# One pass of ScalarE and a rounding copy on VectorE in place of two passes of ScalarE, in a mixture-of-experts kernel

## The chip, the cores and the metric

The kernel runs as one program on one core of a Trainium2 chip. The metric is the device time of the whole program in microseconds (us); lower is better. Beside it stands the span, which is the time from the first to the last instruction in the profiled execution. Five engines work side by side, each through its own list in order: TensorE (PE; its weight loads are shown apart as PEld), VectorE (DVE), ScalarE (ACT), GpSimd (POOL) and SyncE (SP). They wait for each other through semaphores.

## The reference

A modulated linear layer is followed by a mixture of experts with residual. There are T = 8192 tokens with D = 256 features, E = 8 experts with F = 1024 hidden units, the two best experts of each token are taken, and each expert takes at most 2560 tokens.

```python
ys = y * scale
d = jax.lax.rsqrt(jnp.einsum('bi,io->bo', ys * ys, weight * weight) + EPS)
out = jnp.einsum('bsi,io->bso', Efou * ys[:, None, :], weight) * d[:, None, :]
...
logits = x @ wr.T
vals, idx = jax.lax.top_k(logits, TOP_K)
...
xg = x_pad[dispatch]
h = _gelu(jnp.einsum('ecd,edf->ecf', xg, w1) + b1[:, None, :])
y = jnp.einsum('ecf,efd->ecd', h, w2) + b2[:, None, :]
g = g_pad[dispatch, jnp.arange(E)[:, None]]
wy = y * g[..., None]
```

## The kernel before, in words

The first 100 us or so compute the modulated layer and the routing for 16 groups of 512 tokens. Then come 52 blocks, each for one expert. A long block has 3 x 128 gathered tokens (384 columns), a short one 2 x 128 (256 columns). The first blocks, of expert 0, are all long; each later expert has some long blocks and then some short ones. The whole document calls the change from the last long block of an expert to its first short block a seam. There are seven seams, one for each of experts 1 to 7, and their first short blocks start at about 252, 353, 471, 560, 648, 767 and 873 us.

All products run on TensorE in the type fp32r. To keep accuracy a matrix is split in two parts, hi (the value rounded to fp32r) and lo (the value less hi). The hidden layer of a block is made in 8 chunks of 128 hidden units, f = 0 to 7. For each chunk:

- PE makes the first product into one of two PSUM banks, `h_bank` (lines 611 to 613, 6 matmuls), and signals `h_open`.
- ACT (`gelu`, line 853) turns the bank into `h_raw` in full fp32, and once more into `h_hi`, rounded to fp32r. After both it signals `gelu_done`. This lets PE write the bank again (`bank_read`) and lets DVE go on.
- DVE (`split_chunk`, line 1262) computes `h_lo` as `h_raw` less `h_hi`, and signals `h_ready`.
- PE makes the second product with `h_hi` and `h_lo` as stationary operands (lines 625 and 627, in blocks 0 and 1 lines 642 to 645) once `chunk_split` has seen `h_ready`. `h_raw`, `h_hi` and `h_lo` are rings of four.

PE runs ahead: it makes the first product of chunk f before the second product of chunk f - 3, and it opens chunks 0 and 1 of the next block before it ends this one. The order of each engine is written out by hand. On DVE the work between two blocks is: chunk 7 of this block, chunk 0 of the next, then for each 128 tokens an addition of PSUM and bias and a second addition (lines 1290 and 1293, which wait for PE's `y_done` and free PE's output banks through `y_read`), then chunk 1 of the next block, then one multiplication by the gate for each 128 tokens (line 1299, `y_ready`), then chunks 2 to 7. After chunk 6 DVE makes the lo part of the next block's input (line 1247) and copies the gates (line 1256). Chunks 0 and 1 of a block are always split over 384 columns there, also when the block is short. In the first two long blocks of an expert DVE also splits the next expert's weights (line 982) between chunks 2 to 5.

GpSimd gathers the tokens of a later block (line 417), and adds the weighted results to the output in DRAM with indirect DMAs (line 438) after `y_ready`. The landing of those DMAs (`added`) is awaited by the next block's first line 1290.

In block 0 DVE still has routing work between the chunks. It makes the last choice of experts (to line 1025), then chunk 0, the gates (lines 1030 to 1034), chunk 1, the slots (lines 1046 to 1151, which wait for a product of PE), chunk 2, a one-hot list (lines 1076 to 1097), chunks 3 and 4, and so on.

Of the kernel before, what the change touches and what calls it, by code (L numbers as in the profile page):

```python
# [13 lines left out]
ACT = mybir.ActivationFunctionType  # L14
AX_X = mybir.AxisListType.X

P = 128
# [5 lines left out]
FC = F // P  # L23
# [48 lines left out]
RING = 4  # L72
H_BANKS = 2
# [13 lines left out]
def build(nc, x, x_t, cond_t, w, wr_t, w1, b1_t, w2, b2, ident, tri, expert_low, slot_base, middle_ids, lanes, columns,  # L87
# [9 lines left out]
    with ExitStack() as ctx:  # L97
        def sb(name, shape, dt=F32):
            return ctx.enter_context(nc.sbuf_tensor("sb_" + name, shape, dt))

        def sem(name):
            return ctx.enter_context(nc.semaphore(name))
# [19 lines left out]
        b1_now = [sb(f"b1_now{u}", [P, FC]) for u in range(2)]  # L122
# [68 lines left out]
        h_raw = [h_raw_sb[:, i * SLOTS:(i + 1) * SLOTS] for i in range(RING)]  # L191
        h_hi = [sb(f"h_hi{i}", [P, SLOTS], F32R) for i in range(RING)]
# [101 lines left out]
        gelu_done = sem("gelu_done")  # L294
        h_ready = sem("h_ready")
        y_done = sem("y_done")
        y_half = sem("y_half")
        y_read = sem("y_read")
        y_ready = sem("y_ready")
        added = sem("added")  # L300
# [21 lines left out]
        h_bank = [bank[4], bank[5]]  # L322
# [443 lines left out]
        def _(act):  # L766
# [82 lines left out]
            def gelu(u, b, f, subs=SUBS):  # L849

                act.wait_ge(h_open, b * FC + (f + 1))
                for h in (h_raw[f % RING], h_hi[f % RING]):
                    ins = act.activation(h[:, 0:subs * P], h_bank[f % H_BANKS][:, 0:subs * P], ACT.Gelu_apprx_tanh,  # L853
                                         bias=b1_now[u][:, f:f + 1])
                ins.then_inc(gelu_done, 1)

            def one_block(u, e, b, piece0, last=False, subs=SUBS):
                for f in range(FC):
                    gelu(u, b, f, subs)
                    if isinstance(b, int) and b == 0 and f == 1:  # L860
                        odds(SETS - 1)
                    if f == 6 and not last:
                        act.wait_ge(h_open, b * FC + FC)
                        split_rows(b + 1)
                    if piece0 is not None and f in SPLIT_AT:
                        split_piece(1 - u, piece0 + SPLIT_AT.index(f), 32 * (e + 2))
# [34 lines left out]
        def _(dve):  # L901
# [356 lines left out]
            def split_chunk(b, f, subs=SUBS):  # L1258

                cols = slice(0, subs * P)  # L1260
                dve.wait_ge(gelu_done, b * FC + (f + 1))
                dve.tensor_tensor(h_lo[f % RING][:, cols], h_raw[f % RING][:, cols],  # L1262
                                  h_hi[f % RING][:, cols].bitcast(F32), ALU.subtract).then_inc(h_ready, 1)

# [3 lines left out]
            take_gates(0, first=True)  # L1268
            choose(SETS - 1)
            split_chunk(0, 0)  # L1270
            set_gates(SETS - 1)
            split_chunk(0, 1)
            find_slots(SETS - 1)
            list_third_block()
# [40 lines left out]
            def one_block(u, e, b, piece0, last=False, subs=SUBS):  # L1315

                for f in range(2, FC):
                    split_chunk(b, f, subs)
                    if isinstance(b, int) and b < 2 and f in (2, 4):
                        list_group(LAST_SET + 2 * b + f // 2 - 1)  # L1320
                    if isinstance(b, int) and b == 1 and f == 5:
                        base_of_slots()
                    if f == 6 and not last:
                        split_rows(b + 1)
                        take_gates(b + 1, first=isinstance(b, int) and b == 0)
                    if piece0 is not None and f in SPLIT_AT:
                        i = piece0 + SPLIT_AT.index(f)
                        split_piece(1 - u, i, PIECES * (e + 1) + (i + 1))
                if isinstance(b, int) and b == 1:
                    plan_blocks()  # L1330
                if not last:
                    split_chunk(b + 1, 0)
                if isinstance(b, int) and b == 0:
                    dve.wait_ge(b2_in, 16)
                for s in range(subs):
                    if last:
                        last_sum(e, b, s, subs)
                    else:
                        add_bias(e, b, s, subs)
                if not last:  # L1340
                    split_chunk(b + 1, 1)
                    for s in range(subs):
                        weigh(e, b, s, subs)
# [80 lines left out]
```

## Time and profile before

| what | value |
|---|---|
| time, median of 3 runs | 905.96 us (905.81 to 906.36) |
| time of the profiled execution | 906.11 us |
| its span | 904.0 us |
| around the span | 2.1 us |
| granted TensorE clock over the span | 0.997 |
| busy share PE / PEld / DVE / ACT / POOL | 99 / 89 / 59 / 60 / 49 % |
| start of the first block's second products | 113.9 us (chunk 2), 116.6 us (chunk 3) |

The profiled execution's own time is the span and the 2.1 us around it. Busy time of an engine is the union of its instructions, so two that overlap in the pipeline count once. A share of 99% on PE says that PE almost always has a matmul in flight.

### The profile page before, as it was taken

Reading aid. Unit: us, or ns where it says so; the run is one execution under the profiler, and the core shown is the slowest. Engines: PE = TensorE matmul, PEld = TensorE weight load, DVE = VectorE, ACT = ScalarE, POOL = GpSimd, SP = SyncE. Lnnn points to the kernel's source line nnn. Section 1 sums busy time; section 2 is a strip of 40 time slices with the busy share of each in tenths; the row PEclk is TensorE's granted clock in tenths of the full one; section 3 lists DMA queues with packets and bytes.
Section 4 is the critical chain, followed back from the end, with each engine's and each line's share of the span. In section 5 each row is a group of like instructions: output and inputs, shape, how many; then the busy total and the mean of one; then the engine's idle time right before and its main releaser. Section 6 shows DMA issues by size and latency. Waiting matters only on the chain.

```text
span 904.0 us, 18417 instructions
## 1 busy us (share of the span) xinstructions
PE 892.1 (99%) x5605; PEld 807.3 (89%) x5605; DVE 532.2 (59%) x1286; ACT 541.2 (60%) x1290; POOL 445.2 (49%) x472
## 2 busy tenths in 40 slices
PE   9999999999999999999999999999999999999995
PEld 6666899999999999999999999999999999999995
DVE  5789876556455565565455555556456645544543
ACT  4888645656556665666556655666566645655552
POOL 0000324645466545665446654655566544664453
PEclk9999999999999999999999999999999999999998
DMA  9775582522533353333423352335233322342232
GB/s 334 260 255 186 181 298 44 133 62 43 133 54 57 52 139 44 57 64 57 122 42 59 60 133 42 62 54 140 39 57 66 46 44 42 52 67 36 47 42 30
DMA packets 55848, 84.37 MB, mean 93 GB/s; under 512 B 6848, under 2 KB 44880, under 8 KB 55408
## 3 DMA queue, kind: packets, MB, share of 16 engines
q0 software_dynamic: 28592, 38.20, 26.6%
q1 hardware_dynamic: 25632, 44.87, 14.7%
q10 hardware_dynamic: 1568, 0.58, 0.2%
q8 instruction: 32, 0.52, 0.2%
q14 instruction: 24, 0.20, 0.1%
HBM read 53.71 MB, written 38.31 MB: 102 GB/s over the span
## 4 chain that ended last, share of the span: by engine, by line
PE 97%; ACT 1%; DMA 1%; DVE 0%; POOLq 0%; issue 0%; POOL 0%; SPq 0%; ACTq 0%
PE bank L625 26%; PE bank L611 14%; PE bank L612 14%; PE bank L613 14%; PE bank L627 13%; PE bank L514 6%; PE bank L599 3%; PE bank L527 2%; PE bank L529 2%; PE bank L562 1%; PE bank L642 1%; PE bank L644 1%; PE bank L645 1%; DMA sb_x<-in_x_t 1%; POOLq L97 0%
## 5 line engine op out<-in xcount | busy, mean ns | idle before, releaser
L625 PE MATMUL bank<-sb_w_both,sb_h_hi 128*128 128x512 f32 x1000 | 373.8, 402 | 0.0
L853 ACT ACTIVATE sb_h_raw<-bank,sb_b_now 128x384 f32<-128x384 f32 (+1 forms) x416 | 223.6, 538 | 249.4 <-PE bank L613 248.7
L1262 DVE TENSOR_TENSOR sb_h_lo<-sb_h_raw,sb_h_hi 128x384 fp32r<-128x384 f32 (+1 forms) x416 | 209.6, 511 | 226.1 <-ACT sb_h_hi L853 224.3
L438 POOL DMA_INDIRECT out_rows<-sb_y,sb_add_ids x154 | 271.3, 1762 | 125.8 <-DVE sb_y L1299 85.2
L627 PE MATMUL bank<-sb_w_both,sb_h_lo 128*128 128x256 f32 x1000 | 282.1, 282 | 0.0
L611 PE MATMUL bank<-sb_xt_hi,sb_w_both 128*128 128x384 f32 (+1 forms) x832 | 264.6, 318 | 0.2 <-ACT sb_h_hi L853 0.2
L612 PE MATMUL bank<-sb_xt_lo,sb_w_both 128*128 128x384 f32 (+1 forms) x832 | 260.1, 313 | 0.0
L613 PE MATMUL bank<-sb_xt_hi,sb_w_both 128*128 128x384 f32 (+1 forms) x832 | 259.8, 312 | 0.0
L853 ACT ACTIVATE sb_h_hi<-bank,sb_b_now 128x384 fp32r<-128x384 f32 (+1 forms) x416 | 221.0, 531 | 0.0
L625 PEld LDWEIGHTS bank<-sb_w_both,sb_h_hi 128*128 128x128 f32 x1000 | 188.0, 188 | 30.2 <-DVE sb_y L1293 0.2
L627 PEld LDWEIGHTS bank<-sb_w_both,sb_h_lo 128*128 128x128 f32 x1000 | 188.5, 189 | 0.0
L611 PEld LDWEIGHTS bank<-sb_xt_hi,sb_w_both 128*128 128x128 f32 x832 | 156.7, 188 | 20.3 <-DVE sb_xt_lo L1247 0.8
L417 POOL DMA_INDIRECT sb_xg<-hidden,sb_gather_ids x133 | 136.7, 1028 | 70.9 <-POOL sb_ids_ring L413 43.5
L612 PEld LDWEIGHTS bank<-sb_xt_lo,sb_w_both 128*128 128x128 f32 x832 | 156.8, 189 | 0.0
L613 PEld LDWEIGHTS bank<-sb_xt_hi,sb_w_both 128*128 128x128 f32 x832 | 156.4, 188 | 0.0
L410 POOL COPY sb_gather_ids<-sb_ids 128x3 int32 (+2 forms) x52 | 9.9, 190 | 247.5 <-DVE sb_gates L1256 127.7
L1247 DVE TENSOR_TENSOR sb_xt_lo<-bank,sb_xt_hi 128x384 fp32r<-128x384 f32 x104 | 53.1, 552 | 73.4 <-ACT sb_xt_hi L828 73.4
L828 ACT CAST sb_xt_hi<-bank 128x384 fp32r<-128x384 f32 x104 | 44.8, 483 | 78.1 <-PE bank L613 76.4
L1290 DVE TENSOR_TENSOR sb_y<-bank,sb_b 128x256 f32<-128x256 f32 x125 | 52.4, 420 | 31.8 <-PE bank L627 26.8
L514 PE MATMUL bank<-sb_x,sb_w 128*128 128x512 f32 x128 | 57.7, 595 | 0.4 <-DVE sb_x L931 0.4
L1293 DVE TENSOR_TENSOR sb_y<-sb_y,bank 128x256 f32<-128x256 f32 x125 | 52.6, 421 | 5.8
L982 DVE TENSOR_TENSOR sb_w_both<-sb_w_raw,sb_w_both 128x512 fp32r<-128x512 f32 x64 | 44.0, 688 | 3.5 <-ACT sb_w_both L796 3.4
(148 smaller groups left out, 620.7 us busy)
## 6 DMA issues: line engine op xcount, KB each, us to landing
sb_w_raw<-in_w SPq DMA_DIRECT2D x16, 1024.0 KB, 9.6
hidden<-sb_rows SPq DMA_DIRECT2D x4, 2112.0 KB, 10.3
sb_x<-in_x_t SPq DMA_DIRECT2D x16, 512.0 KB, 5.7
out_rows<-in_x SPq DMA_DIRECT2D x16, 512.0 KB, 7.5
out_rows<-sb_y,sb_add_ids POOLq DMA_INDIRECT x155, 3.9
sb_xg<-hidden,sb_gather_ids POOLq DMA_INDIRECT x133, 2.8
sb_b<-in_b SPq DMA_DIRECT2D x1, 1024.0 KB, 9.7
hidden<-sb_empty SPq DMA_DIRECT2D x4, 132.0 KB, 8.0
```

The costliest lines, as they stand in the source:

```text
L417: pool.indirect_dma_start(xg[:, s, :], None, hidden[0:PAD + sets * TS * P, :], bass.IndirectOffsetOnAxis(gather_ids[:, s:s + 1], axis=0),) ...
L438: pool.indirect_dma_start(out, bass.IndirectOffsetOnAxis(add_ids[:, s:s + 1], axis=0), y[s][:, :], None, compute_op=ALU.add,).then_inc(add ...
L514: mm = pe.matmul(m_bank[c % M_RING][:, :], w_sb[:, k, o * P:(o + 1) * P], x_in[g % X_RING][:, k, :], start=(k == 0), stop=(k == KC - 1))
L611: pe.matmul(h, w_hi[u][:, cols], xt_hi[:, rows], start=(k == 0), stop=False)
L612: pe.matmul(h, w_hi[u][:, cols], xt_lo[:, rows], start=False, stop=False)
L613: mm = pe.matmul(h, w_lo[u][:, cols], xt_hi[:, rows], start=False, stop=(k == KC - 1))
L625: pe.matmul(wide_bank[s][:, :].rearrange("p (v d) -> p v d", v=2), hi, w_both[u][:, :, cols], start=(f == 0), stop=False, skip_group_check ...
L627: mm = pe.matmul(wide_bank[s][:, 0:D], lo, w_hi[u][:, cols], start=False, stop=(f == FC - 1), skip_group_check=True)
L853: ins = act.activation(h[:, 0:subs * P], h_bank[f % H_BANKS][:, 0:subs * P], ACT.Gelu_apprx_tanh, bias=b1_now[u][:, f:f + 1])
L1247: dve.tensor_tensor(xt_lo[:, rows_k], x_bank[k][:, 0:SLOTS], xt_hi[:, rows_k].bitcast(F32), ALU.subtract).then_inc(xt_ready, 1)
L1262: dve.tensor_tensor(h_lo[f % RING][:, cols], h_raw[f % RING][:, cols], h_hi[f % RING][:, cols].bitcast(F32), ALU.subtract).then_inc(h_read ...
L1293: dve.tensor_tensor(y[s][:, :], y[s][:, :], wide_bank[s][:, D:2 * D], ALU.add).then_inc(y_read, signals(s, subs))
```

## The change

In `gelu` ScalarE makes one pass in place of two. It writes `h_raw` alone and signals `gelu_done` after it. In `split_chunk` VectorE first copies `h_raw` into `h_hi`, which rounds it to fp32r, and signals a new semaphore `hi_made`. It waits for this semaphore itself and then takes the difference as before. Nothing else is changed; the lines behind the new ones move by one.

```diff
         y_half = sem("y_half")
+        hi_made = sem("hi_made")
         y_read = sem("y_read")
...
                 act.wait_ge(h_open, b * FC + (f + 1))
-                for h in (h_raw[f % RING], h_hi[f % RING]):
-                    ins = act.activation(h[:, 0:subs * P], h_bank[f % H_BANKS][:, 0:subs * P], ACT.Gelu_apprx_tanh,
-                                         bias=b1_now[u][:, f:f + 1])
-                ins.then_inc(gelu_done, 1)
+                act.activation(h_raw[f % RING][:, 0:subs * P], h_bank[f % H_BANKS][:, 0:subs * P], ACT.Gelu_apprx_tanh,
+                               bias=b1_now[u][:, f:f + 1]).then_inc(gelu_done, 1)
...
                 dve.wait_ge(gelu_done, b * FC + (f + 1))
+                dve.tensor_copy(h_hi[f % RING][:, cols], h_raw[f % RING][:, cols]).then_inc(hi_made, 1)
+                dve.wait_ge(hi_made, b * FC + (f + 1))
                 dve.tensor_tensor(h_lo[f % RING][:, cols], h_raw[f % RING][:, cols],
                                   h_hi[f % RING][:, cols].bitcast(F32), ALU.subtract).then_inc(h_ready, 1)
```

On DVE, between two blocks, the program has these rows before: the last pair of additions, chunk 1 of the next block, and the multiplications by the gates.

```order
L1290 TENSOR_TENSOR sb_y<-bank,sb_b 128x256 [waits y_done]
L1293 TENSOR_TENSOR sb_y<-sb_y,bank 128x256 [waits y_half]
L1261 REGISTER_ALU
L1262 TENSOR_TENSOR sb_h_lo<-sb_h_raw,sb_h_hi 128x384 [waits gelu_done]
L1298 REGISTER_ALU
L1299 ISA [waits y_read]
L1299 TENSOR_SCALAR sb_y<-sb_y,sb_gates 128x256
```

After the change the same place of the same engine reads so; the copy is listed as CAST.

```order
L1291 TENSOR_TENSOR sb_y<-bank,sb_b 128x256 [waits y_done]
L1294 TENSOR_TENSOR sb_y<-sb_y,bank 128x256 [waits y_half]
L1260 REGISTER_ALU
L1261 CAST sb_h_hi<-sb_h_raw 128x384 [waits gelu_done]
L1263 TENSOR_TENSOR sb_h_lo<-sb_h_raw,sb_h_hi 128x384 [waits hi_made]
L1299 REGISTER_ALU
L1300 ISA [waits y_read]
L1300 TENSOR_SCALAR sb_y<-sb_y,sb_gates 128x256
```

One instruction is put in ahead of each difference, with no further register instruction, and what follows on DVE stands behind both.

## Rows read from the trace of the kernel before

**Rows 1.** The page: busy time by engine, and the chain that ended last.
```profile
PE 892.1 (99%) x5605; PEld 807.3 (89%) x5605; DVE 532.2 (59%) x1286; ACT 541.2 (60%) x1290; POOL 445.2 (49%) x472
...
PE 97%; ACT 1%; DMA 1%; DVE 0%; POOLq 0%; issue 0%; POOL 0%; SPq 0%; ACTq 0%
```

**Rows 2.** The page's groups, ScalarE's two passes: busy us, mean ns, idle before.
```profile
L853 ACT ACTIVATE sb_h_raw<-bank,sb_b_now 128x384 f32<-128x384 f32 (+1 forms) x416 | 223.6, 538 | 249.4 <-PE bank L613 248.7
...
L853 ACT ACTIVATE sb_h_hi<-bank,sb_b_now 128x384 fp32r<-128x384 f32 (+1 forms) x416 | 221.0, 531 | 0.0
```

**Rows 3.** Groups of VectorE by shape, over the whole span.
```profile
L1262 DVE TENSOR_TENSOR sb_h_lo<-sb_h_raw,sb_h_hi 128x384 fp32r<-128x384 f32 x278 | 153.2, 556 | 168.4 <-ACT sb_h_hi L853 167.3 <-issue 0.2 <-DVE sb_rows L1034 0.2
L1262 DVE TENSOR_TENSOR sb_h_lo<-sb_h_raw,sb_h_hi 128x256 fp32r<-128x256 f32 x138 | 56.4, 423 | 57.7 <-ACT sb_h_hi L853 57.1
...
L1299 DVE TENSOR_SCALAR sb_y<-sb_y,sb_gates 128x256 f32<-128x256 f32 x131 | 40.1, 356 | 0.0
...
L914 DVE TENSOR_SCALAR sb_ys_t<-sb_ys_t 128x256 f32<-128x256 f32 x1 | 0.3, 294 | 3.0 <-DMA sb_ys_t<-in_cond_t 3.0
...
L976 DVE CAST sb_tri<-sb_tri_f 128x128 bf16<-128x128 f32 x1 | 0.2, 219 | 0.0
```

**Rows 4.** Timeline of VectorE in block 0: start us, us, what.
```profile
108.49 0.56 DVE L1262 TENSOR_TENSOR sb_h_lo<-sb_h_raw,sb_h_hi 128x384 fp32r<-128x384 f32 x1 [0.15 <-DVE sb_rows L1034]
109.58 0.29 DVE L1046 TENSOR_SCALAR sb_over<-bank 128x128 f32<-128x128 f32 x1 [0.53 <-PE bank L548]
...
113.26 0.55 DVE L1262 TENSOR_TENSOR sb_h_lo<-sb_h_raw,sb_h_hi 128x384 fp32r<-128x384 f32 x1
...
115.69 1.02 DVE L1262 TENSOR_TENSOR sb_h_lo<-sb_h_raw,sb_h_hi 128x384 fp32r<-128x384 f32 x2
```

**Rows 5.** Timeline, block 0, first weight load of chunks 2 and 3.
```profile
113.86 0.19 PEld L642 LDWEIGHTS bank<-sb_w_both,sb_h_hi 128*128 128x128 f32 x1 [0.33 <-DVE sb_h_lo L1262]
...
116.64 0.19 PEld L642 LDWEIGHTS bank<-sb_w_both,sb_h_hi 128*128 128x128 f32 x1
```

**Rows 6.** Timeline of VectorE at the second seam.
```profile
352.54 0.42 DVE L1290 TENSOR_TENSOR sb_y<-bank,sb_b 128x256 f32<-128x256 f32 x1
352.99 0.42 DVE L1293 TENSOR_TENSOR sb_y<-sb_y,bank 128x256 f32<-128x256 f32 x1
353.33 0.55 DVE L1262 TENSOR_TENSOR sb_h_lo<-sb_h_raw,sb_h_hi 128x384 fp32r<-128x384 f32 x1
353.80 0.87 DVE L1299 TENSOR_SCALAR sb_y<-sb_y,sb_gates 128x256 f32<-128x256 f32 x3
354.58 0.42 DVE L1262 TENSOR_TENSOR sb_h_lo<-sb_h_raw,sb_h_hi 128x256 fp32r<-128x256 f32 x1
```

**Rows 7.** Timeline, second seam, first weight load of chunks 1 and 2.
```profile
354.20 0.19 PEld L625 LDWEIGHTS bank<-sb_w_both,sb_h_hi 128*128 128x128 f32 x1
...
355.61 0.19 PEld L625 LDWEIGHTS bank<-sb_w_both,sb_h_hi 128*128 128x128 f32 x1
```

**Rows 8.** Timeline at the first seam, chunk 1: VectorE, then its weight load.
```profile
252.85 0.55 DVE L1262 TENSOR_TENSOR sb_h_lo<-sb_h_raw,sb_h_hi 128x384 fp32r<-128x384 f32 x1
...
253.57 0.19 PEld L625 LDWEIGHTS bank<-sb_w_both,sb_h_hi 128*128 128x128 f32 x1
```

**Rows 9.** Timeline, short block behind a short block, chunk 1 likewise.
```profile
364.92 0.55 DVE L1262 TENSOR_TENSOR sb_h_lo<-sb_h_raw,sb_h_hi 128x384 fp32r<-128x384 f32 x1
...
366.13 0.19 PEld L625 LDWEIGHTS bank<-sb_w_both,sb_h_hi 128*128 128x128 f32 x1
```

**Rows 10.** Timeline, last add behind the second seam; the line 1290 that awaits it.
```profile
359.04 1.57 POOL L438 DMA_INDIRECT out_rows<-sb_y,sb_add_ids  x1 [0.30 <-issue]
...
363.27 0.42 DVE L1290 TENSOR_TENSOR sb_y<-bank,sb_b 128x256 f32<-128x256 f32 x1 [0.33 <-PE bank L627]
```

**Rows 11.** The page's DMA issues: count, median us from issue to landing.
```profile
out_rows<-sb_y,sb_add_ids POOLq DMA_INDIRECT x155, 3.9
```

**Rows 12.** Timeline, a gather's issue under two of line 1299.
```profile
791.24 0.65 DVE L1299 TENSOR_SCALAR sb_y<-sb_y,sb_gates 128x256 f32<-128x256 f32 x2
...
791.29 0.95 POOL L417 DMA_INDIRECT sb_xg<-hidden,sb_gather_ids  x1 [0.30 <-issue]
```

## The prediction

> **What bounds the kernel now.** I first read the busy shares and the chain of waits. PE has a matmul in flight for 99% of the span and holds 97% of the chain; ACT and DVE hold 1% or less of it, though each is busy for 60% [rows 1]. So what ACT saves is worth nothing by itself. PE never waits for `gelu_done` except once near 106 us, for about 0.3 us, before other waits end. The change can only matter where it makes PE wait. So the second thing I read, block by block, is how long before the first weight load of each second product its `h_lo` is ready. I call this the slack of the chunk. The weight load is the place to look, since it loads `h_hi`, the part that `chunk_split` guards.
>
> Most slacks are large: 0.9 to 5 us. Three kinds of place are tight, all where DVE has other work in a row, so that chunks stand in its queue with their activation long done:
>
> - Block 0. Chunk 2 is ready at 113.26 + 0.55 = 113.81, and PE loads at 113.86 after an idle 0.33 us that DVE ended: PE already waits there. It starts 0.04 us after the release, which I use as the time to wake up. The pair of chunks 3 and 4 begins at 115.69, so chunk 3 is ready at about 116.25, against a load at 116.64: slack 0.39 [rows 4, 5].
> - The seams. Chunk 1 stands behind six additions. At the second seam it is ready at 353.33 + 0.55 = 353.88 against 354.20: slack 0.32. Chunk 2 is ready at 355.00 against 355.61: slack 0.61 [rows 6, 7]. At the first seam chunk 1 has 253.57 - 253.40 = 0.17 [rows 8]. The other five are like the second to within 0.05 us.
> - A short block behind a short one: chunk 1 has 366.13 - 365.47 = 0.66 [rows 9], the same in all of them, and chunk 2 some 1.2.
>
> **The change part by part.** ACT loses 416 passes, 221.0 us [rows 2]. That is off PE's path. Where DVE waits for ACT, the chunk's latency hardly moves: the second pass goes (0.53 us of record, some 0.1 less in the pipeline) and a copy of nearly that length comes. These are the 226 us in which DVE now idles for `h_hi` [rows 3], so there the copy is hidden in the time that ACT gives back. Where the activation is long done and DVE is behind, as in the three places above, the whole copy is added.
>
> The price of the copy. No row has an fp32 copy of 384 columns. One bound is two elements a cycle: a scaling in SBUF takes 294 ns for 256 columns, and a cast 219 for 128 [rows 3]. That is 75 ns for 128 columns more, so 384 columns are some 0.36 us. The other bound is the rate of the two-operand difference, 556 ns for 384 and 423 for 256 [rows 3]. I take 0.36 and 0.29, because the copy is like the cast and the scaling: one source, both sides in SBUF. The difference then waits for the copy's own semaphore. The pair of lines 1290 and 1293 shows such a wait: 352.54 + 0.42 = 352.96, and the next starts at 352.99 [rows 6], so 0.03 to 0.05. The sum is **0.40 us for a chunk of 384 columns, 0.33 for 256** (by the other bound 0.60 and 0.46). DVE gets 278 x 0.40 + 138 x 0.33 = 157 us more work and stays below 80% busy.
>
> The Trainium skill has the same on the rate ("VectorE: DVE Perf Modes", the perf-mode tier table): a copy from SBUF to SBUF in fp32 runs at two elements a cycle, a tensor_tensor at one. It says nothing of fp32r as the output type.
>
> Term 1, block 0. Chunks 0 and 1 get a copy each, 0.80. The difference of chunk 1 ends at 109.05, and DVE then idles 0.53 us for PE before line 1046 (0.61 from where it could start, as operations behind each other overlap by 0.08) [rows 4]. So the slots start 0.80 - 0.61 = 0.2 later. The copy of chunk 2 adds 0.40, so PE waits 0.6 longer for chunk 2. Chunk 3 becomes ready 0.2 + 0.4 + 0.4 = 1.0 later, and with its slack of 0.39 and the waking this moves PE to 1.0 - 0.39 + 0.04 = 0.65 in all. Chunks 4 to 7 have over 2 us and absorb the rest. **+0.65 us.**
>
> Term 2, the seams. At the second one chunk 1 is ready 0.40 later: 0.40 - 0.32 + 0.04 = 0.12 of waiting. The three multiplications behind it move by 0.40 too, and chunk 2 has a copy of 256: 0.73 later, 0.73 - 0.61 + 0.04 = 0.16 in all. Chunk 3 has about 2 us. So 0.16 for six seams, and 0.40 - 0.17 + 0.04 = 0.27 for the first (with its chunk 2: 0.33). 6 x 0.16 + 0.33 = **+1.3 us.**
>
> Costed at nothing: the short blocks (0.40 against 0.66; if the copy cost 0.60 its cover would be just gone), the additions of lines 1290 and 1293, which wait for PE after an idle of 0.33 [rows 10] while chunk 0's chain stays as long as it was, and the copy in the last block, where it takes the place of a pass. `y_ready` comes 0.40 later because the multiplications stand behind chunk 1. GpSimd's adds wait for it, and the next line 1290 for their landing. This is closest behind a seam: the last add is issued at 359.04 and lands 3.9 later (median), at 362.94, against 363.27 [rows 10, 11]. That is 0.33, and PE has itself moved by 0.16, so 0.40 just fits. I add **0.1** for this and for the first gather behind the block plan, which PE meets with about 0.1 to spare.
>
> Sum: 0.65 + 1.3 + 0.1 = 2.05 us. The profiled execution took 906.11 (span 904.0), 0.15 above the median of 905.96, so the sum gives 908.16 from the one and 908.0 from the other; I forecast **908.1 us**. About 0.2% (1.8 us) is what a measurement of this kernel can tell from no change, so the forecast stands close to that line, on its slower side.
>
> **The rivals.**
>
> A, not slower: the copy is covered nearly whole. Three of line 1299 take 0.87 [rows 6], so such operations start 0.26 apart. If the difference could start 0.26 behind the copy and not 0.40, block 0 would cost 0.26 (two copies, 0.52, stay below the 0.61), the seams nothing (0.26 against 0.32 and 0.46 against 0.61), and the first seam 0.13. Sum 0.4: 906.5 us. It decides at about 0.30 for the copy and its wait. Against it: the dependent pair 1290 and 1293 starts only after the end.
>
> B, the copy runs at one element a cycle, because its output is fp32r: 0.60 and 0.46. Block 0: 1.2 - 0.61 + 0.6 = 1.2 at chunk 2, and 1.8 - 0.39 + 0.04 = 1.45 at chunk 3. A seam: 1.06 - 0.61 + 0.04 = 0.5, the first 0.65, in all 3.65. With 0.3 for the plan's gather the sum is 5.4: 911.5 us. Against it are the cast and the scaling of [rows 3]; for it only that none of them writes fp32r.
>
> C, the copies hold up GpSimd. If its DMAs could not be issued while a copy runs, the three adds behind a seam (about 5.5 us, some four copies of 0.29) would end 1.2 us later, plus the 0.40 of `y_ready`. Less the 0.33 the next line 1290 is 1.2 us late, and PE stands still for nearly all of that, since its output banks come free late. Seven seams: 8 us more, 916 us. The row nearest to it speaks against it: a gather's issue under 0.65 us of two scalings took 0.95 [rows 12], which is as short as such an issue gets.
>
> The Trainium skill ("SBUF — State Buffer", SBUF: two separate sides) states the rule behind C: an operation of DVE in a two-port mode, as an fp32 copy in SBUF is, locks GpSimd out of the shared port, and it can then write no descriptors. By that rule line 1299 should lengthen the issue, and here it doesn't.
>
> **How the numbers follow.** The forecast has 0.60, A 0.12, B 0.14, C 0.10; 0.04 is left for something that makes it faster by over 0.2%, for which I see no mechanism, as PE is at work throughout. The forecast's own range is 907.1 to 909.2, by 0.3 or 0.45 for the copy and its wait. It crosses the line of 907.8, and I put 0.2 of its 0.60 below. Same: 0.20 + 0.12 + 0.02 = 0.34. Slower: 0.40 + 0.14 + 0.08 = 0.62. The range that holds 8 in 10 reaches from A to B, 906.5 to 911.7, and leaves out C and the faster rest.
>
> **What would show it.** The copy's group should have 278 of some 0.36 us and 138 of 0.29, ACT's busy time should fall by 220 us and DVE's rise by about 150. The list of waits should have PE's weight loads waiting for `h_lo` at 114 and 117 us and at the seams, in all 1 to 2 us more, and nowhere else. A copy of 0.55 would say B; issues of line 438 longer than now, or line 1290 waiting for landings at seven places, would say C. I am wrong altogether if PE's matmuls change their pace, or if waits turn up in the short blocks.

## The result, and the profile after

The changed kernel takes 910.53 us (median of 4 runs, 910.52 to 911.22) against 905.91 us for the kernel before (4 runs, 905.81 to 906.36): a ratio of 1.005, with a 95% interval of 1.0039 to 1.0062. It is 4.6 us slower. The profiled execution has a span of 908.4 us against 904.0, 4.4 us more, at a granted clock of 0.996.

The page, with the busy time by engine and the chain that ended last, answers to [rows 1]:

```profile
PE 895.3 (99%) x5605; PEld 809.2 (89%) x5605; DVE 670.7 (74%) x1702; ACT 367.4 (40%) x874; POOL 437.4 (48%) x472
...
PE 92%; DVE 3%; issue 2%; DMA 1%; ACT 1%; POOLq 0%; POOL 0%; DVEq 0%; ACTq 0%
...
L853 ACT ACTIVATE sb_h_raw<-bank,sb_b_now 128x384 f32<-128x384 f32 (+1 forms) x416 | 223.0, 536 | 403.7 <-PE bank L614 403.7
```

ACT lost 173.8 us of busy time and not 221: passes that ran into each other were counted once where they overlapped. DVE gained 138.5 us. PE's share of the chain fell from 97% to 92%. The groups of VectorE by shape answer to [rows 3]:

```profile
L1263 DVE TENSOR_TENSOR sb_h_lo<-sb_h_raw,sb_h_hi 128x384 fp32r<-128x384 f32 x278 | 156.4, 563 | 9.6
L1261 DVE CAST sb_h_hi<-sb_h_raw 128x384 fp32r<-128x384 f32 x278 | 104.9, 377 | 74.0 <-ACT sb_h_raw L853 68.9 <-issue 4.7 <-DVE sb_rows L1033 0.2
...
L1261 DVE CAST sb_h_hi<-sb_h_raw 128x256 fp32r<-128x256 f32 x138 | 43.4, 315 | 10.8 <-ACT sb_h_raw L853 8.2 <-issue 1.2
```

The copy is a CAST in the trace. It takes 377 and 315 ns in the mean, 0.35 and 0.29 us where nothing disturbs it. The two-operand difference takes 0.56 and 0.43, so the copy runs at the faster of the two rates that the prediction weighed, as forecast. "issue" is idle time that no wait explains; the difference had 0.2 us of it before, the copy has 5.9.

To find where 4.4 us went I took, for each block, the first weight load of chunk 0's second product, and compared it with the same load before:

| stretch | change, us | forecast |
|---|---|---|
| start of the span to block 0 | -0.56 | 0 |
| block 0 | +1.09 | +0.65 |
| blocks 1 and 2 (the gather behind the plan) | +0.16 | 0.1 with `y_ready` |
| seven seams: 0.31, 0.30, 0.47, 0.31, 0.30, 0.59, 0.40 | +2.68 | +1.3 |
| short blocks 9 to 11 | +0.36 | 0 |
| blocks 44, 45 | +0.21 | 0 |
| all other blocks (none over 0.03) | 0.0 | 0 |
| last block to the end | +0.46 | 0 |

The second seam on VectorE, against [rows 6]:

```profile
354.32 0.42 DVE L1294 TENSOR_TENSOR sb_y<-sb_y,bank 128x256 f32<-128x256 f32 x1
354.66 0.35 DVE L1261 CAST sb_h_hi<-sb_h_raw 128x384 fp32r<-128x384 f32 x1
355.05 0.56 DVE L1263 TENSOR_TENSOR sb_h_lo<-sb_h_raw,sb_h_hi 128x384 fp32r<-128x384 f32 x1
355.52 0.87 DVE L1300 TENSOR_SCALAR sb_y<-sb_y,sb_gates 128x256 f32<-128x256 f32 x3
356.44 0.29 DVE L1261 CAST sb_h_hi<-sb_h_raw 128x256 fp32r<-128x256 f32 x1
356.77 0.43 DVE L1263 TENSOR_TENSOR sb_h_lo<-sb_h_raw,sb_h_hi 128x256 fp32r<-128x256 f32 x1
```

Chunk 1 is as forecast: its difference starts 355.05 - 354.66 = 0.39 later than it would. Then look at what starts behind the multiplications. They end at 355.52 + 0.87 = 356.39, and the copy starts at 356.44, 0.05 after. In [rows 6] the next operation starts at 354.58, 0.09 *before* the end at 354.67. Of a seam's 0.31, chunk 1 has 0.13 and chunk 2 has 0.18, where the forecast had 0.12 and 0.04. So about 0.14 a seam is time that no instruction of the sum accounts for.

PE's weight loads by what they waited for (total us, times, longest; waits under 0.15 are not listed, so most of the seams don't show):

```profile
PEld bank L643 <- DVE sb_h_lo L1263: 1.8, 2, 1.3
...
PEld bank L612 <- DVE sb_xt_lo L1246: 1.6, 8, 0.4
...
PEld bank L626 <- DVE sb_h_lo L1263: 0.7, 3, 0.3
```

The first line is block 0: two waits of 1.8 together, where the kernel before had two of 0.9. The second is for the lo part of the next block's input; its longest, 0.4, stands in block 43 and comes up again below.

### The profile page after: what moved, and what is told of

Its sections match the earlier page's. It is cut to its first block, busy times and chain, and to the rows that moved or that the text cites. A ratio compares the mean times of both kernels' runs of the same rounds, so it can differ in the third digit from the quotient of the medians.

```text
span 908.4 us, 18417 instructions
## 1 busy us (share of the span) xinstructions
PE 895.3 (99%) x5605; PEld 809.2 (89%) x5605; DVE 670.7 (74%) x1702; ACT 367.4 (40%) x874; POOL 437.4 (48%) x472
## 4 chain that ended last, share of the span: by engine, by line
PE 92%; DVE 3%; issue 2%; DMA 1%; ACT 1%; POOLq 0%; POOL 0%; DVEq 0%; ACTq 0%
PE bank L626 26%; PE bank L612 13%; PE bank L628 13%; PE bank L613 13%; PE bank L614 13%; PE bank L515 6%; PE bank L600 3%; PE bank L528 2%; PE bank L530 2%; PE bank L563 1%; PE bank L495 1%; DVE sb_h_lo L1263 0%; DMA out_rows<-sb_y,sb_add_ids 0%; DMA sb_xg<-hidden,sb_gather_ids 0%; POOLq L97 0%
## 5 line engine op out<-in xcount | busy, mean ns | idle before, releaser
L439 POOL DMA_INDIRECT out_rows<-sb_y,sb_add_ids x154 | 257.6, 1672 | 133.6 <-DVE sb_y L1300 93.0
L1263 DVE TENSOR_TENSOR sb_h_lo<-sb_h_raw,sb_h_hi 128x384 fp32r<-128x384 f32 (+1 forms) x416 | 215.5, 518 | 14.3
L1261 DVE CAST sb_h_hi<-sb_h_raw 128x384 fp32r<-128x384 f32 (+1 forms) x416 | 148.3, 357 | 84.8 <-ACT sb_h_raw L853 77.0
L418 POOL DMA_INDIRECT sb_xg<-hidden,sb_gather_ids x133 | 139.4, 1048 | 70.9 <-POOL sb_ids_ring L414 43.5
```

Of the source, the lines that this page charges most:

```text
L418: pool.indirect_dma_start(xg[:, s, :], None, hidden[0:PAD + sets * TS * P, :], bass.IndirectOffsetOnAxis(gather_ids[:, s:s + 1], axis=0),) ...
L439: pool.indirect_dma_start(out, bass.IndirectOffsetOnAxis(add_ids[:, s:s + 1], axis=0), y[s][:, :], None, compute_op=ALU.add,).then_inc(add ...
L1261: dve.tensor_copy(h_hi[f % RING][:, cols], h_raw[f % RING][:, cols]).then_inc(hi_made, 1)
```

## The experiments

My theory after the result: (1) the copy costs only where VectorE is already late, and not by how many copies there are; (2) at a seam it costs 0.4 us of work, less the slack, and 0.14 more, because the difference waits for an instruction of VectorE itself: that holds its sequencer, which then can't do the loop's bookkeeping for chunk 2 ahead of time; (3) the tail's 0.46 comes from `y_ready`. All runs are compared with the kernel before on the same chip; its medians there were 906.49, 906.23 and 906.41.

**e1, chunk 1 back on ScalarE.**

```diff
+                for h in (h_raw[f % RING], h_hi[f % RING]) if f == 1 else (h_raw[f % RING],):
...
+                if not (f == 1):
+                    dve.tensor_copy(h_hi[f % RING][:, cols], h_raw[f % RING][:, cols]).then_inc(hi_made, 1)
+                    dve.wait_ge(hi_made, b * (FC - 1) + max(f, 1))
```

> The changed kernel, but ScalarE again makes both passes for chunk 1 of every block (no copy and no wait on hi_made there); the other seven chunks keep the copy. Theory: of the 4.4 us that the change cost, 2.7 came at the seven seams and 0.5 at the tail, and both come from the copy of chunk 1 that stands behind the additions (it makes chunk 1 and y_ready 0.40 late and takes VectorE's head start before chunk 2). Then the seams cost at most 0.5 together, the last landing is waited for no longer than before (0.16 us), and the time is about 907.2 (906.6 to 907.8). Rival: the copies cost by how many there are (work on VectorE, use of SBUF), wherever they stand; with 52 of 416 gone only an eighth of 4.4 us comes back, about 910.0.

Measured 907.07 us (10 runs), ratio 1.0009 (0.9999 to 1.0018), span 904.9. All seven seams cost 0.00, blocks 9 to 11, 44 and 45 nothing either, and the last block -0.04. Block 0 and the stretch ahead of it come to +0.18. What is left is block 2, which grew by 0.69, and block 3 by 0.15: PE's transposes waited for the gather behind the plan. So one copy in eight made most of the loss, 3.4 of the 4.4 us by the profiles, and the count theory (910.0) is out. The multiplications behind chunk 1 and the first copy of chunk 2:

```profile
354.79 0.87 DVE L1303 TENSOR_SCALAR sb_y<-sb_y,sb_gates 128x256 f32<-128x256 f32 x3
355.58 0.29 DVE L1264 CAST sb_h_hi<-sb_h_raw 128x256 fp32r<-128x256 f32 x1
```

355.58 is 0.08 before their end at 355.66. With neither the copy nor the self-wait ahead of it, the overlap is back; e1 alone can't tell which of the two took it.

**e2, block 0 back on ScalarE.** The condition is `isinstance(b, int) and b == 0` in place of `f == 1`; in block 0 ScalarE's first pass counts `hi_made` up in the copy's place.

> The changed kernel, but ScalarE makes both passes in block 0 only. Theory: block 0 lost 1.09 us against its own start, through the copies of chunks 0 to 3 in front of and between the slot plan's operations; without them that comes back and everything behind it moves 0.6 to 1.1 us earlier: 909.4 to 909.9 us, with the seams as in the changed kernel. Rival: PE's wait in block 0 has another end behind it (the gathers of the plan), and the gain is given back by block 3: 910.3 to 910.6.

Measured 909.56 us, ratio 1.0038 (1.0024 to 1.0052), span 907.4: inside the theory's interval. Block 0 grew by 0.01, but block 2, with PE's wait for its gather, grew by 0.34 where the changed kernel had 0.21. The seams cost 0.31 to 0.34 but for block 23's 0.67, and the last block 0.55.

**e3, the kernel before with a wait of VectorE on itself.**

```diff
                 dve.wait_ge(gelu_done, b * FC + (f + 1))
+                dve.memset(tiny_sb[:, :], 0.0).then_inc(tiny_made, 1)
+                dve.wait_ge(tiny_made, b * FC + (f + 1))
```

> The kernel before, but VectorE writes one column (a memset of 128x1 that nothing reads) ahead of each difference, and the difference waits for that memset's own semaphore. It adds the wait on VectorE itself with hardly any of the copy's work. Theory: a wait on an instruction of VectorE itself holds its sequencer, so that the loop's bookkeeping before chunk 2 starts only when chunk 1's difference has been sent; then chunk 2's first instruction starts up to 0.1 us after the end of the multiplications and no longer 0.08 before it, and the seams cost 0.05 to 0.15 us each; time 906.2 to 907.5. Rival: the extra at chunk 2 comes from the copy's length; then chunk 2's first instruction still starts 0.08 before the end and each seam is as before to within 0.03 beyond what the memset itself lasts, time 905.9 to 906.4.

Measured 907.07 us (10 runs), ratio 1.0006 (0.9996 to 1.0015), span 904.5. The time can't be told from that of the kernel before; what follows rests on the trace. The second seam:

```profile
353.37 0.06 DVE L1264 MEMSET sb_tiny<- 128x1 f32 x1
353.48 0.56 DVE L1266 TENSOR_TENSOR sb_h_lo<-sb_h_raw,sb_h_hi 128x384 fp32r<-128x384 f32 x1
353.95 0.87 DVE L1303 TENSOR_SCALAR sb_y<-sb_y,sb_gates 128x256 f32<-128x256 f32 x3
354.91 0.06 DVE L1264 MEMSET sb_tiny<- 128x1 f32 x1
```

The multiplications end at 354.82, and the next operation starts at 354.91, 0.09 after the end, where it was 0.09 before the end. Work of 0.06 us did that, so it isn't the copy's length. That it isn't the additional instruction either is for e7 to show. The gap is 0.07 to 0.09 at five seams and 0.18 to 0.20 at two, those of blocks 23 and 50. In the changed kernel it is 0.04 to 0.06 at five and 0.17 and 0.15 at the same two, which is why these cost 0.47 and 0.40 there. In the kernel before it was -0.08, and -0.05 once. Counted over the seven seams the changed kernel lost 1.1 us of head start. Here the seams themselves cost 0.01 to 0.07 each, less than I expected: chunk 2's difference ends 355.43 - 353.00 = 2.43 behind the start of the last addition, where it was 355.00 - 352.99 = 2.01, and the slack of 0.61 covers these 0.42. The rest of the 0.5 us by which this profile is longer stands in block 0 (0.18), blocks 18 and 19 (0.18) and the last block (0.12).

**e7, the copy of chunk 1 ahead of the last pair of additions.** `round_chunk` is the copy with its wait for `gelu_done`; the wait on `hi_made` stays ahead of the difference.

```diff
                 for s in range(subs):
+                    if not last and s == subs - 1:
+                        round_chunk(b + 1, 1, slice(0, SUBS * P))
...
-                    split_chunk(b + 1, 1)
+                    split_chunk(b + 1, 1, rounded=True)
```

> The changed kernel, but chunk 1's copy is issued before the last pair of additions instead of behind it; the work on VectorE is the same and the copy still stands in the same row, only its semaphore is long up when chunk 1's difference comes. Theory of the sequencer: chunk 1 is as late as in the changed kernel, but VectorE's head start is back, chunk 2's copy starts 0.08 before the end of the multiplications, and each seam costs about 0.15 less: 909.4 us (909.0 to 909.8). Rival: the loss at the seams is the copy's length alone and no matter of order: 910.3 to 910.7.

Measured 912.95 us, ratio 1.0073 (1.0056 to 1.009), span 910.8: slower than the changed kernel, which neither side expected. Yet the seams did what the theory says, and more: 0.03 to 0.09 at five of them in place of about 0.31, and 0.34 and 0.33 at blocks 43 and 50.

```profile
355.91 0.42 DVE L1299 TENSOR_TENSOR sb_y<-sb_y,bank 128x256 f32<-128x256 f32 x1
356.25 0.55 DVE L1268 TENSOR_TENSOR sb_h_lo<-sb_h_raw,sb_h_hi 128x384 fp32r<-128x384 f32 x1
356.72 0.87 DVE L1305 TENSOR_SCALAR sb_y<-sb_y,sb_gates 128x256 f32<-128x256 f32 x3
357.51 0.29 DVE L1260 CAST sb_h_hi<-sb_h_raw 128x256 fp32r<-128x256 f32 x1
```

The copy starts 0.08 before the end of the multiplications at 357.59: the head start is back, with the same instructions in the row and no wait that is still open in front of the difference. The loss is elsewhere. Block 2 grew by 1.07, since the three issues of its gather took 1.42, 1.30 and 1.29 (more on this under e5). Fifteen short blocks grew by 0.2 to 0.5 each, and PE's weight loads there waited for the last addition:

```profile
PEld bank L626 <- DVE sb_y L1299: 4.7, 15, 0.4
```

I had counted the slack of `h_lo` and not that of the additions. In short blocks it is smaller than the copy is long.

The sequencer's own records at the second seam, first the kernel before, then the changed one, e3 and e7 (counts, min/median/max ns, first and last start):

```profile
L1299 DVEq FUSED_REGOPS  x3: 65/71/140, 353.2 to 353.7; - x3
```
```profile
L1300 DVEq FUSED_REGOPS  x3: 65/71/140, 355.1 to 355.7; - x3
```
```profile
L1303 DVEq FUSED_REGOPS  x3: 65/71/140, 353.6 to 354.1; - x3
```
```profile
L1305 DVEq FUSED_REGOPS  x3: 65/71/140, 356.0 to 356.6; - x3
```

The first register operation comes 0.6 us ahead of the first multiplication before (353.2 against 353.80), 0.4 in the changed kernel (355.1, 355.52), 0.35 in e3 (353.6, 353.95) and 0.7 in e7 (356.0, 356.72). This lead is what the self-wait takes and the early copy gives back. Behind the multiplications come the registers and the branch of the loop. In the changed kernel the last of them is the second of these two, which starts at 356.34 and lasts 0.06; the copy of chunk 2 starts at 356.44, 0.05 after its end:

```profile
L1352 DVEq FUSED_REGOPS  x2: 63/120/177, 356.1 to 356.3; - x2
```

The record at which the lead begins shows the same. In the kernel before, the sequencer's record for the first multiplication starts 0.21 us ahead of the difference (353.12 against 353.33). In the changed kernel the sequencer's first record behind the difference starts 0.01 us after the difference itself has started (355.06 against 355.05), so it stood still while the difference waited for the copy.

**e4, the copy at the rate of the difference.**

```diff
-                dve.tensor_copy(h_hi[f % RING][:, cols], h_raw[f % RING][:, cols]).then_inc(hi_made, 1)
+                dve.tensor_tensor(h_hi[f % RING][:, cols], h_raw[f % RING][:, cols], h_raw[f % RING][:, cols],
+                                  ALU.max).then_inc(hi_made, 1)
```

> The changed kernel with the copy replaced by a tensor_tensor of the same result (the larger of h_raw and h_raw), which takes one element per cycle: 0.56 us for 384 columns and 0.43 for 256 instead of 0.36 and 0.29. Theory (what counts is how late VectorE is where it is late already): at each seam 0.20 + 0.14 more, so 0.6 to 0.7 per seam instead of 0.35, block 0 0.4 to 0.6 more, some short blocks begin to wait: 913.5 to 916 us. And if the copies in the changed kernel are lengthened by a port that VectorE shares with GpSimd, this operation, which needs both sources and never leaves GpSimd out, is lengthened differently: its records beside GpSimd's instructions are within 0.03 us of those without. Rival: PE has cover for another 0.2 us, 910.5 to 911.5.

Measured 916.57 us, ratio 1.0113 (1.0097 to 1.0128), span 915.0. The groups by shape:

```profile
L1261 DVE TENSOR_TENSOR sb_h_hi<-sb_h_raw 128x384 fp32r<-128x384 f32 x278 | 154.1, 554 | 53.5 <-ACT sb_h_raw L853 48.9 <-issue 4.2 <-DVE sb_rows L1033 0.2
...
L1261 DVE TENSOR_TENSOR sb_h_hi<-sb_h_raw 128x256 fp32r<-128x256 f32 x138 | 57.8, 419 | 3.5 <-ACT sb_h_raw L853 1.3 <-issue 0.8
```

Six seams cost 0.62 to 0.76 and block 43's has 0.96, blocks 0 to 2 together 3.26. So 0.20 us more on each copy of 384 columns and 0.13 on one of 256 made 6 us more, slightly over what I expected. The mean of 554 ns is that of the undisturbed difference, 556 [rows 3]. The 83 of these operations that lay wholly within an issue of GpSimd took 0.55 to 0.59, those beside none 0.55 to 0.56, so this form is hardly lengthened. The additional 0.03 at most is just what the expectation allowed.

**e5, e1 and e2 together.** The condition is `f == 1 or (isinstance(b, int) and b == 0)`; 357 copies are left (not 317, as I wrote below before the run).

> The two undone parts together: ScalarE makes both passes in block 0 and for chunk 1 of every block, the copy does the rest (317 of 416 chunks). Theory: the copies that are left stand where VectorE waits for ScalarE, so they cost nothing: as the kernel before, 905.9 to 906.6 us, with no wait of PE for h_lo beyond the kernel before's. Rival: the parts overlap and block 3 (the first gather behind the block plan) gives 0.3 to 0.8 back: 906.6 to 907.2.

Measured 906.98 us (11 runs), ratio 1.0009 (1.0 to 1.0018): the rival's number, not the theory's. Block 0 grew by 0.07 and the seams by nothing, but block 2 grew by 0.73. (Two later blocks, 16 and 39, have a jump of 0.33 each, of the kind described under b2.) The three issues of the gather behind the plan, and VectorE's copies at the same time:

```profile
148.64 1.42 POOL L418 DMA_INDIRECT sb_xg<-hidden,sb_gather_ids  x1 [0.84 <-POOL sb_ids_ring L414]
150.36 1.30 POOL L418 DMA_INDIRECT sb_xg<-hidden,sb_gather_ids  x1 [0.30 <-issue]
151.97 1.29 POOL L418 DMA_INDIRECT sb_xg<-hidden,sb_gather_ids  x1 [0.30 <-issue]
...
149.66 0.55 DVE L1266 CAST sb_h_hi<-sb_h_raw 128x384 fp32r<-128x384 f32 x1
...
151.33 0.51 DVE L1266 CAST sb_h_hi<-sb_h_raw 128x384 fp32r<-128x384 f32 x1
```

Both sides are lengthened: the copies by 0.16 to 0.20, and the issues, which took 1.19, 1.10 and 0.95 in the kernel before, in sum by 0.77.

**e8, the early copy only in long blocks.** The condition of e7 becomes `early and s == subs - 1`, with `early = subs == SUBS and not isinstance(b, int)`.

> The changed kernel, but chunk 1's copy stands before the last pair of additions only where the loop over long blocks issues it (so at the seams too), and behind them in short blocks and in blocks 0 and 1. The version with the early copy everywhere had the seams at 0.07 us each but every short block 0.2 to 0.3 later, because PE waited there for the last additions. Theory: seams 0.07 and short blocks as in the changed kernel, in sum 1.7 us less than the changed kernel: about 908.8 us (908.4 to 909.2). Rival: the delay of the additions shows behind the long blocks too, or the next block gives the seam's gain back: 910 us or more.

Measured 908.79 us, ratio 1.0026 (1.0016 to 1.0037), as the theory gave. Four seams cost 0.03 to 0.05 and two 0.09; block 43 has 0.32, block 9 keeps its 0.29 and the last block has 0.66. This is 1.7 us faster than the changed kernel with the same work on every engine.

**e10, the change in the first chunk alone.** The kernel before, with one pass and a copy for chunk 0 of block 0.

> The kernel before with the change in one chunk alone, chunk 0 of block 0, where PE waits for ScalarE's second pass (0.5 us by the list of waits) and VectorE has 0.6 us idle behind it. Theory: the start of block 0's second products moves 0.2 to 0.4 us earlier and block 0 keeps it, 905.5 to 905.8 us, which only the trace can tell from the kernel before. Rival: the slot plan behind it is 0.4 later and PE gives it all back in block 0: 905.9 to 906.1.

Measured 906.39 us against 906.23, ratio 1.0002 (0.9993 to 1.0011). Block 1 started 0.16 us earlier, which is about what two profiles of one kernel differ by (0.09, below). It beats nothing that can be measured.

**e11, no copy beside that gather.** e5, with `b < 3` in place of `b == 0`.

> The version with both parts undone, and ScalarE also makes both passes in blocks 1 and 2, so that no copy stands beside the first gather behind the block plan (block 3's, issued during block 2). Theory: a copy beside a gather's issue lengthens both; the three issues of that gather take 3.2 us again as in the kernel before, not 4.0, PE waits for it less than 0.2 us, and block 3 starts as in the kernel before: 906.1 to 906.4 us, 0.6 to 0.8 less than with copies in blocks 1 and 2. Rival: the gather starts late for another reason (the index copy of GpSimd ahead of it came 0.25 later too), and its issues are long because of the additions and differences beside them: block 3 still starts 0.5 or more later and the time stays at 906.8 to 907.1.

```profile
147.98 1.18 POOL L418 DMA_INDIRECT sb_xg<-hidden,sb_gather_ids  x1 [0.84 <-POOL sb_ids_ring L414]
149.47 1.10 POOL L418 DMA_INDIRECT sb_xg<-hidden,sb_gather_ids  x1 [0.30 <-issue]
150.87 0.95 POOL L418 DMA_INDIRECT sb_xg<-hidden,sb_gather_ids  x1 [0.30 <-issue]
```

The issues take 3.23 us again, blocks 2 and 3 start no later than before, and the time is 906.43 us (11 runs) against 906.41, ratio 0.9998 (0.9989 to 1.0007). Its profile isn't wholly without growth: it began block 0 0.31 earlier than the kernel before and then lost 0.43 over blocks 9 to 11, where PE waited for an addition, as in the jumps described under b2. In this version 343 of 416 chunks have the copy, and within the interval, 0.8 us to either side, it costs nothing. It also gains nothing, since PE bounds it.

**a2 and b2, both kernels once more.**

> The changed kernel once more, for how far the parts of its loss repeat from one profile to the next. Theory: what has a fixed cause repeats to 0.05 us: seams at 0.30 each (the ones at blocks 23 and 43, which had 0.47 and 0.59, fall to 0.3), block 0 at 1.0 to 1.1, the last landing 0.4 to 0.5 later. Rival: the seams' extra is chance; then they scatter between 0 and 0.6.

> The kernel before once more, for the same reason: its block starts should repeat within 0.05 us from block 1 to the end, but for single jumps of about 0.3 where an addition waits for a late landing; if the stretch ahead of block 0 differs by 0.2 or more, the changed kernel's earlier start by 0.56 is partly chance.

a2 took 910.74 us, ratio 1.0046 (1.003 to 1.0061), span 908.5. Its seams are 0.29, 0.30, 0.45, 0.34, 0.30, 0.59 and 0.39, block 9 has 0.31 again, the end 0.56, a little over the 0.4 to 0.5 expected. I had expected the long ones at blocks 23 and 43 to fall to 0.3; they didn't, so they have a fixed cause too. b2 (one run, 907.4, span 905.2) started block 0 0.09 later than the first profile and has two jumps, 0.45 at block 7 and 0.48 at block 21. Such jumps come now and then in versions on the old timing. At both, the additions ahead had waited 2.0 to 2.1 for the landing of an add, and PE then waited 0.5 for the additions. e10 has the same at block 14, but its jumps at blocks 4 and 28 have PE's wait for the additions without a late landing in the list. Its line of the landings:

```profile
DVE sb_y L1294 <- DMA out_rows<-sb_y,sb_add_ids: 6.6, 4, 1.9
```

I take these jumps for the reason why the kernel before scatters by a microsecond and more; no experiment shows it.

## Why the prediction was right, and where it was too small

Its range, 906.5 to 911.7, holds the 910.53, and the sign and the main places were right. The sum was 2.05 us and the measured loss 4.6, so terms were too small, and one was missing. That the range still holds the time is in part luck: its upper half was there for rival B, a slower copy, and that is not what happened. The forecast's own range, 907.1 to 909.2, ends 1.3 us short. One sign of being wrong also came up, a wait in a short block (block 9).

- **Price of the copy, right.** 0.36 and 0.29 forecast, 0.35 and 0.29 undisturbed. With its wait 0.39 against 0.40.
- **Term 1, block 0, right in its end.** +0.65 forecast; block 1 started 0.52 later. Block 0 itself grew by 1.09, because it began 0.56 earlier and VectorE, not PE, sets when its chunk 2 is ready. e2 confirms it. Of the 0.56 about 0.3 is PE's wait for ScalarE near 106 us, which went away. The whole repeats in a2 (0.51), but e5 and e11, which are alike up to there, start block 0 at +0.10 and -0.31, so a part can be chance. I can't assign it.
- **Term 2, the seams, mis-sized: 2.68 against 1.3.** Chunk 1's part was exact (0.13 against 0.12). The step that failed is "chunk 2 has a copy of 256: 0.73 later". It left out that a wait of VectorE on itself also costs the head start: 0.12 to 0.23 a seam, 1.1 in all, of the 1.4 that were missing; another 0.29 is block 43's, which has another cause, below. e3 shows the loss of the head start with the wait and a memset of 0.06 us, e7 and e8 take it away by order alone. The slack of the first seam I had taken too small: chunk 1 cost 0.13 there and not 0.27, since in the profile of before a pause of 0.14 stood among its additions. That is no chance: b2 has the same pause to 0.01, and no version with another code has it.
- **The short blocks, costed at nothing.** Right for most: at chunk 1, 0.17 to 0.23 is left of 0.66. Block 9's 0.31 at chunk 2 repeats in a2 (and in e8), and it is the head start once more, only larger:

```profile
266.37 0.61 DVE L1300 TENSOR_SCALAR sb_y<-sb_y,sb_gates 128x256 f32<-128x256 f32 x2
267.40 0.29 DVE L1261 CAST sb_h_hi<-sb_h_raw 128x256 fp32r<-128x256 f32 x1 [0.41 <-ACT sb_h_raw L853]
```

The copy starts 0.41 after the end of the multiplications. The activation named there is that of a later chunk; chunk 2's had ended at 265.15. And e3, with its memset in place of the copy, has a gap of 0.45 at the same place. What is longer is the sequencer's part: at two places 0.41 and 0.29 us pass between one of its records and the next, where the kernel before has 0.05 and 0.14. e2, where block 9 starts 0.45 earlier, doesn't have these pauses, and its gap is 0.06. Why they come stays open.
- **Block 43's other 0.29** has nothing to do with chunk 2. It stands at chunk 6, where PE waits 0.40 and not 0.12 for the lo part of the next block's input, since ScalarE's cast of that input starts 0.28 later. The changed kernel, then e2, which has no such loss:

```profile
776.47 0.86 ACT L829 CAST sb_xt_hi<-bank 128x384 fp32r<-128x384 f32 x2 [1.73 <-PE bank L614]
```
```profile
775.71 0.86 ACT L829 CAST sb_xt_hi<-bank 128x384 fp32r<-128x384 f32 x2 [1.45 <-PE bank L614]
```

PE and the record of ScalarE's sequencer ahead of the cast stand at the same distance from the block's start in both, to 0.01. So this too is a pause in front of one instruction, here on ScalarE. It repeats in a2, e4, e7 and e8 and is absent in the other versions; its cause stays open.
- **The last block, missing: +0.46.** I looked at `y_ready` behind a seam, where it just fits, and not at the end, where the last block's scaling waits for the landing. Before, then after:

```profile
892.71 0.35 DVE L1308 TENSOR_SCALAR sb_y<-sb_b,sb_gates 128x256 f32<-128x256 f32 x1 [0.16 <-DMA out_rows<-sb_y,sb_add_ids]
```
```profile
897.18 0.35 DVE L1309 TENSOR_SCALAR sb_y<-sb_b,sb_gates 128x256 f32<-128x256 f32 x1 [0.73 <-DMA out_rows<-sb_y,sb_add_ids]
```

The wait grew by 0.57. Not all of it is `y_ready`, which came 0.39 later by the block's own start. The issue of the first add behind it also took longer. Before, then after:

```profile
886.75 1.58 POOL L438 DMA_INDIRECT out_rows<-sb_y,sb_add_ids  x1 [1.06 <-DVE sb_y L1299]
```
```profile
891.08 1.80 POOL L439 DMA_INDIRECT out_rows<-sb_y,sb_add_ids  x1 [1.61 <-DVE sb_y L1300]
```

The 1.80 comes again in a2, e2 and e8 (1.78 to 1.80), and every other version has 1.56 to 1.59. The growth is gone in e1, where `y_ready` is on time and the issue takes 1.57, and stays in e2.

- **Rival A** is out: the difference does not start until the copy has ended. **Rival B**'s time was nearer to the result than my own, by a wrong mechanism: e4 is B, and it costs 10.3 us more than the kernel before, not 5.4, because blocks 1 and 2 (1.34), the short blocks, the head start and the last block come on top. Its condition did not hold here, since the copy takes 0.35.
- **Rival C** was wrong at its places and too lightly argued from [rows 12]. GpSimd's adds are not longer (1672 ns in the mean, before 1762), but copies and issues do lengthen each other. At one gather with no slack, that cost 0.7 to 0.8 us in e1 and e5. In the changed kernel itself, the same three issues happened to fall so that they took 1.09, 1.10 and 1.13. The rule that I weighed there (the Trainium skill, "SBUF — State Buffer", SBUF: two separate sides) is an exclusive lock: of a two-port operation of VectorE and an instruction of GpSimd, whichever starts first holds the shared port for its whole length, and the other is fully blocked. The traces bear it out in part. e5 against e11 shows that the two get into each other's way. But a copy that starts within an issue should then stand still until the issue ends. In the changed kernel 71 copies of 384 columns lie wholly within the issue of an add: 54 of them took 0.39 us or less, nearly the undisturbed 0.35, and the other 17 took 0.58 to 0.65, far short of the end of an issue of about 1.6. All 17 started 0.63 to 0.91 us into the issue, as did only one of the others.

## What to carry to other kernels

Work that moves to an engine with 40% of its time free still costs its length, less the slack, where that engine has a row of ready work with a consumer behind it: find those places, and take the slack of everything that stands behind in the row (here chunk 1, chunk 2, the additions and the last landing), not of the next result alone. A wait on an instruction of the same engine costs more than the gap it makes, since nothing behind it is prepared meanwhile; with other work put between the two, the same instructions cost 0.03 to 0.09 us at six of the seven seams of e8 instead of 0.30 to 0.47. And move only the part that has cover: 343 of 416 chunks moved at no cost that the times can show, and the other 73 made the 4.6 us.

## What the hardware showed that I had not expected

- A wait of VectorE on its own last instruction delays work that stands some instructions further on, behind loop bookkeeping, by 0.12 to 0.26 us at the seams (a memset of 0.06 us in e3 is enough to wait for), and by 0.5 at block 9, where the sequencer also paused.
- An fp32 copy in SBUF beside an indirect DMA's issue on GpSimd: in e5 0.51 and 0.55 us in place of 0.35, and the issues 1.29 to 1.42 in place of 0.95 to 1.19. It depends on the moment: most copies within an issue kept their length, and those that started 0.63 to 0.91 us into the issue of an add took up to 0.65. The two-operand form of e4 took 0.59 at most, against 0.55 undisturbed.
- The sequencers of VectorE and ScalarE pause for 0.2 to 0.4 us at a few places, which change from one version to another and not from one profile to the next: block 9, and block 43 on ScalarE.
- Waits of a few tenths repeat from one execution to the next: the seams agree to 0.03 us in the two profiles of the changed kernel, while those on the old timing differ by jumps of 0.3 to 0.5.
